# A two-layer graph kernel on one core: the first row gathers and two weight loads moved from the relation block into the projection block ahead of it

## What is computed

```
seg  = edge_type * n + dst
agg  = segment_sum(x[src], seg, num_segments=N_REL * n)
cnt  = segment_sum(ones, seg, num_segments=N_REL * n)
mean = agg.reshape(N_REL, n, -1) / maximum(cnt, 1.0).reshape(N_REL, n, 1)
h1   = einsum('rni,rio->no', mean, W_rel) + x @ W_root + b_rgcn
xw   = h1 @ W_gcn
```

## Time and profile before

| what | value |
|---|---|
| median of 3 runs | 1698.77 us (1698.74 to 1700.25) |
| the profiled execution's own time | 1700.29 us |
| its span in the trace | 1698.5 us |
| TensorE's mean granted clock | 0.861 of full |
| PE busy (matrix products) | 1337.8 us, 79% of the span |
| DVE busy | 935.5 us, 55% |
| POOL busy | 634.3 us, 37% |
| ACT busy | 535.3 us, 32% |
| 36-product groups of the relation block (L599 on r_pO) | 2592 products, 433.1 us |

### The profile page before, as it was taken

How to read it: one execution, slowest core, us unless ns; L and a number is a source line. 1 busy time by engine, 2 the same in 40 slices (tenths; PEclk the granted TensorE clock), 3 DMA queues, 4 the chain that set the end, 5 groups by cost and what they waited for, 6 DMA issues and landing times. The chain is left out here.

```text
span 1698.5 us, 31020 instructions
## 1 busy us (share of the span) xinstructions
PE 1337.8 (79%) x9640; PEld 983.5 (58%) x9641; DVE 935.5 (55%) x1715; ACT 535.3 (32%) x800; POOL 634.3 (37%) x752
## 2 busy tenths in 40 slices
PE   8699376782846599956799999999999617847988
PEld 6477366782624466845566666666666416434666
DVE  8953867784544542062466665666665145656820
ACT  0000320872221342041455554555554132022300
POOL 0077536775664000012355555555555302110000
PEclk9899595795858599968899999999999858857989
DMA  1000200001002220052899899899998545232401
GB/s 54 1 2 1 77 7 10 1 1 56 19 10 76 75 69 6 1 220 96 282 277 273 267 285 286 229 285 284 288 288 229 139 146 167 65 111 71 157 15 32
DMA packets 103970, 210.46 MB, mean 124 GB/s; under 512 B 23331, under 2 KB 48384, under 8 KB 103789
## 3 DMA queue, kind: packets, MB, share of 16 engines
q1 hardware_dynamic: 75244, 145.72, 24.7%
q0 software_dynamic: 28672, 64.04, 16.6%
HBM read 196.71 MB, written 37.22 MB: 138 GB/s over the span
## 5 line engine op out<-in xcount | busy, mean ns | idle before, releaser
L599 PE MATMUL r_pO<-ring,r_rowsT 128*128 x2592 | 433.1, 326 | 0.0
L599 PEld LDWEIGHTS r_pO<-ring,r_rowsT 128*128 128x128 f16 x2592 | 250.7, 98 | 158.4 <-issue 0.2
L1660 DVE SCALAR_TENSOR_TENSOR ring<-q_wstage,ring 128x768 f16<-128x768 f32 x198 | 175.1, 954 | 67.1 <-ACT ring L1619 65.8
L1599 POOL DMA_INDIRECT acc_dram<-r_msg,r_scol x72 | 133.7, 1858 | 169.4 <-PE r_pT L1720 109.5
L1619 ACT ACTIVATE ring<-q_wstage 128x768 f16<-128x768 f32 x198 | 148.8, 829 | 39.8 <-issue 24.9
L442 POOL DMA_INDIRECT inv_col<-qinv_dram,pair_col x112 | 120.7, 1078 | 79.3 <-POOL pair_col L455 75.2
L392 POOL DMA_INDIRECT slot_dram<-table_record,table_rowi x80 | 105.8, 1323 | 107.8 <-issue 107.2
L355 PE MATMUL acc<-oh_d,oh_s 125*125 125x512 f16 (+1 forms) x800 | 140.6, 315 | 0.0
L1648 ACT ACTIVATE r_msg<-r_pO,slot_inv 128x768 f32<-128x768 f32 x72 | 64.5, 896 | 197.0 <-PE r_pO L599 196.6
L1720 PE MATMUL r_pT<-r_S,q_parts 128*128 128x128 f16 x876 | 104.3, 222 | 26.9 <-DVE r_S L1677 10.8
L1667 DVE TENSOR_TENSOR r_rowsT<-r_pT,r_rowsT 128x512 f16<-128x512 f32 x73 | 50.3, 689 | 126.4 <-ACT r_rowsT L1628 126.4
(11 more groups left out here) (356 smaller groups left out, 2420.9 us busy)
## 6 DMA issues: line engine op xcount, KB each, us to landing
q_wstage<-in_L_gnn_W_rel_dram SPq DMA_DIRECT2D x33, 2304.0 KB, 14.3
f_stage<-in_L_ffn_w_dram SPq DMA_DIRECT2D x12, 768.0 KB, 5.2
stage<-in_L_gnn_W_dram SPq DMA_DIRECT2D x6, 768.0 KB, 6.0
q_wstage<-in_L_ffn_w_fast_dram SPq DMA_DIRECT2D x6, 768.0 KB, 5.3
q_wstage<-in_L_ffn_w_slow_dram SPq DMA_DIRECT2D x6, 768.0 KB, 7.9
q_wstage<-in_L_ffn_h_fast_dram SPq DMA_DIRECT2D x6, 768.0 KB, 9.6
f_stage<-in_L_ffn_w_fast_dram SPq DMA_DIRECT2D x6, 768.0 KB, 4.5
f_stage<-in_L_ffn_w_slow_dram SPq DMA_DIRECT2D x6, 768.0 KB, 6.0
```

The costliest lines, as they stand in the source:

```text
L599: ins = eng.matmul(out, x, w[:, h * n:(h + 1) * n], start=first and x is xh and w is wh, stop=last and x is xl, **kw)
L1599: eng.indirect_dma_start(out=K.acc_dram[u % 2], out_offset=bass.IndirectOffsetOnAxis(ap=scol[:, u:u + 1], axis=0), in_=msg[:, u, :], in_of ...
L1660: ins_ = eng.scalar_tensor_tensor(wring[:, slot, 1, k, :], wstage[:, slot, k, :], W_SCALE, wring[:, slot, 0, k, :], ALU.mult, ALU.subtract)
```

## The change

The helper functions of the relation block that load weights and gather rows move into a class `Relation`, made ahead of the projection block, with their semaphores. The four first gathers are now issued by POOL within the projection block, once the stores of `store_rows` have landed and the transposes are copied out. The loads of W_rel[1] and W_rel[2] are issued by SP within the projection block, behind the store to `xn_dram`, each when the weights that stood in its slot have been cut. The relation block starts its loads with W_rel[3]. The core of the diff:

```diff
+class Relation:
...
+    def load_w(self, eng, r, u):
...
+    def gather(self, eng, t, b):
+
+        idx = self.K.slot_idx
+        eng.tensor_copy(self.gcol[:, b, :], idx[:, t, :] if isinstance(t, int) else idx[:, bass.ds(t, 1), :].rearrange("p a b -> p (a b)")
+                        ).then_inc(self.s_col, 1)
+        eng.wait_ge(self.s_col, t + 1)
+        eng.nop(nofuse=True)
+        eng.indirect_dma_start(out=self.rows[0][:, b, :], out_offset=None, in_=self.K.xn_dram,
...
         @block.sync
         def _(eng):
             eng.dma_start(K.acc_dram[0][0:N, :].rearrange("(i p) c -> p i c", p=P), h1[:, :, :]).then_inc(s["seeded"], 16)
-            for b in range(AHEAD):
-                eng.wait_ge(gathered[b], 32)
-            load_w(eng, 1, 1)
-            with eng.Fori(1, REL // 2) as i:
+            eng.wait_ge(s["w_lo"], 2)
+            relation.load_w(eng, 3, 1)
+            with eng.Fori(2, REL // 2) as i:
                 for u in range(2):
                     eng.wait_ge(s["w_lo"], i * 2 + (u - 1))
-                    load_w(eng, i * 2 + u, u)
+                    relation.load_w(eng, i * 2 + u, u)
...
             eng.sem_inc(s["w_hi"], KC)
             eng.sem_inc(s["w_lo"], 1)
-            for b in range(AHEAD):
-                gather(b, b)
             for u in range(UN):
                 step(u, u, True)
...
             eng.wait_ge(T.s["lo_ready"], NT)
             eng.dma_start(K.xn_dram.rearrange("(i p) c -> p i c", p=P), parts[:, :, :, :].rearrange("p i a c -> p i (a c)")).then_inc(s["extra"], 16)
+            w_root.ready(eng, KC - 1)
+            relation.load_w(eng, 1, 1)
+            w_first.ready(eng, KC - 1)
+            relation.load_w(eng, 2, 0)
             eng.wait_ge(s["extra"], 32)
             eng.wait_ge(s["dumped"], 48)
 
-        def zero_seconds(eng, s):
+        def first_gathers(eng, T, s):
             eng.memset(rows_b[:, :, :], 0.0).then_inc(s["zeroed"], 1)
+            eng.wait_ge(s["dumped"], 48)
+            eng.wait_ge(s["extra"], 32)
+            T.wait_done(eng)
+            for b in range(AHEAD):
+                relation.gather(eng, b, b)
```

More of the change, by code:

```diff
@@ L1406, in _ @@
             else:
-                gpsimd(eng, s)
+                gpsimd(eng, T, s)
         @block.vector
@@ L1503, in scalar, with __init__, relation_phase @@
         eng.activation(self.parts[:, 0, c, :], self.slot(c)[:, 0, :], ACT.Copy, scale=W_SCALE).then_inc(self.s_hi, 1)
-def relation_phase(K, wstage, wring, rows_a, rows_b, h1, w_gcn, merged):
+class Relation:
+    def __init__(self, K, wstage, rows_a, rows_b, gcol):
+        self.K, self.wstage, self.rows, self.gcol = K, wstage, (rows_a, rows_b), gcol
+        self.s_staged = [K.sem("r_staged_%d" % u) for u in range(2)]
+        self.s_col = K.sem("r_col_ready")
+        self.s_gathered = [K.sem("r_gathered%d" % u) for u in range(UN)]
+    def load_w(self, eng, r, u):
+        w_rel = self.K.ins["L1_gnn_W_rel"]
+        eng.dma_start(self.wstage[:, u, :, :], w_rel[r].rearrange("(k p) n -> p k n", p=128) if isinstance(r, int) else
+                      w_rel[bass.ds(r, 1), :, :].rearrange("a (k p) n -> p (a k) n", p=128)).then_inc(self.s_staged[u], 16)
+    def gather(self, eng, t, b):
[5 more added lines that the diff above has]
+        eng.indirect_dma_start(out=self.rows[0][:, b, :], out_offset=None, in_=self.K.xn_dram,
+                               in_offset=bass.IndirectOffsetOnAxis(ap=self.gcol[:, b, 0:1], axis=0)).then_inc(self.s_gathered[b], 16)
+        eng.indirect_dma_start(out=self.rows[1][:, b, :], out_offset=None, in_=self.K.xn_dram,
+                               in_offset=bass.IndirectOffsetOnAxis(ap=self.gcol[:, b, 1:2], axis=0),
+                               bounds_check=N - 1, oob_is_err=False).then_inc(self.s_gathered[b], 16)
+def relation_phase(K, wstage, wring, relation, h1, w_gcn, merged):
     nc, ins = K.nc, K.ins
-    w_rel = ins["L1_gnn_W_rel"]
+    rows, gathered = relation.rows, relation.s_gathered
     with ExitStack() as ctx:
         sb = lambda n, s, d: K.sb(n, s, d, ctx)
-        rows = (rows_a, rows_b)
         rowsT = sb("r_rowsT", [128, 2, 2, KC, 128], FP16)
@@ L1573, in _ @@
         def _(eng):
-            def gather(t, b):
-                eng.tensor_copy(gcol[:, b, :], pair(K.slot_idx, t)).then_inc(s["col_ready"], 1)
-                eng.wait_ge(s["col_ready"], t + 1)
-                eng.nop(nofuse=True)
-                eng.indirect_dma_start(out=rows[0][:, b, :], out_offset=None, in_=K.xn_dram,
-                                       in_offset=bass.IndirectOffsetOnAxis(ap=gcol[:, b, 0:1], axis=0)).then_inc(gathered[b], 16)
-                eng.indirect_dma_start(out=rows[1][:, b, :], out_offset=None, in_=K.xn_dram,
-                                       in_offset=bass.IndirectOffsetOnAxis(ap=gcol[:, b, 1:2], axis=0),
-                                       bounds_check=N - 1, oob_is_err=False).then_inc(gathered[b], 16)
             def step(t, u, first):
@@ L1588, in step @@
                 eng.nop(nofuse=True)
-                gather(t + AHEAD, b)
+                relation.gather(eng, t + AHEAD, b)
                 if first and u == 0:
@@ L1842, in rgcn_phase @@
         merged = MergedFirst(K, wstage[:, :, :, :].rearrange("p s k n -> p s (k n)").rearrange("p s (a n) -> p s a n", a=3))
-        with ExitStack() as relation:
-            rows_b = K.sb("q_rows_b", [128, UN, 2 * C], FP16, relation)
-            project_block(K, "q1", xn, norm, xT, parts, w_root, h1, store_rows, add_bias, beside=w_first, gpsimd=zero_seconds)
+        with ExitStack() as relation_ctx:
+            rows_b = K.sb("q_rows_b", [128, UN, 2 * C], FP16, relation_ctx)
+            relation = Relation(K, wstage, rows_a, rows_b, K.sb("q_gcol", [128, UN, 2], I32, relation_ctx))
+            project_block(K, "q1", xn, norm, xT, parts, w_root, h1, store_rows, add_bias, beside=w_first, gpsimd=first_gathers)
             w_gcn = Weights(K, "q2_w", rows_view(ins["L1_gnn_W_gcn"]), wstage[:, 0], None)
-            relation_phase(K, wstage, wring, rows_a, rows_b, h1, w_gcn, merged)
+            relation_phase(K, wstage, wring, relation, h1, w_gcn, merged)
         w_gcn.parts = sb("gcn_parts", [128, 2, KC, C], FP16)
```

11 lines of the change are left out of this document (2 added, 9 removed).

## The result

The change measured **1694.42 us** (median of 12 executions, all but one disturbed one between 1681.33 and 1696.87), beside 1699.41 for the kernel before (12 executions, 1697.41 to 1703.72): a ratio of 0.9951, 95% interval 0.993 to 0.9972. So it is faster by 5 us where 19.9 were forecast, and outside the range. The time of the profiled execution is 1696.87 us, its span 1694.6.

What follows compares the result with a forecast made beforehand. PE (TensorE) was taken to bound the steady loop, so an earlier start is kept: tile 5's mean 19.9 us earlier, after term 3's 2.4 back, gives 1698.77 - 19.9 = 1678.9 us; range 1675 to 1687.

Steps and rivals of the forecast that it cites:

- Term 1: Relation block's start: with the first gathers issued early, the first mean starts 10.0 us earlier.
- Term 2: Cut of W_rel[1]: early loads remove the wait, so tile 2's products come 21.4 us earlier than before.
- Term 3: First scatter: it now waits for the store of h1, delaying tile 5's mean and giving back 2.4 us.
- rival 1: Store of h1 lands as late as before, delaying the first scatter: gain 13.1 us, 1685.7 us; chance 0.12.
- rival 2: Projection block: early loads stretch the store to xn_dram by 10.4 us: gain 15.2 us, 1683.6 us; chance 0.08.
- rival 4: Projection block: POOL's gather issues stretch beside DVE's work and end the block late: slower, 1705 us; chance 0.04.
- rival 3: Loop of relations: weight loads set the pace and swallow the head start: gain 0 to 3 us, 1698.8; chance 0.04.
- and keeps it, as nothing behind it is changed: Behind tile 5's mean: the 19.9 us gained by there last to the kernel's end.
- More than 7 us of PE waits in the loop: Loop of relations: a listed sign that the forecast is wrong.

Runs made afterwards that it cites:

- e4_other_half: The change, with tile 0 scattering into the accumulator half that the h1 store doesn't touch, and tile 1 waiting for that store instead: 1682.76 us, ratio 0.9895.
- e3: The change with only the two weight loads moved early; the gathers are issued in the relation block as in the kernel before: 1689.7 us, ratio 0.9933.
- e2: The change with only the four gathers moved early; the two weight loads go back to the relation block: 1696.1 us, ratio 0.9978.
- e7: The change with only the gathers of tiles 0 and 1 in the projection block; those of tiles 2 and 3 open the relation block: 1682.47 us, ratio 0.9896.
- e12: The change, with each loop scatter of tile t held until the high part of tile t+2 is written: 1709.15 us, ratio 1.0005.
- e14: The change with two tiles' gathers moved, tile 0 scattering into the other half, and scatters held for tile t+2's high part: 1706.46 us, ratio 0.9981.
- e15: The change with three tiles' gathers moved, tile 0 scattering into the other half, and scatters held for tile t+2's high part: 1702.86 us, ratio 0.9968.

## Why the prediction was wrong, and where it was right

**Term 1 was right.** From the block's start to the products of tile 0 it is 5.6 us, before 16.0: 10.4 won, 10.0 forecast. I had assumed that the first mean runs at the clock's lower level (1.2 GHz) from its start. It began at the higher one and was at the lower by 796, so the products start 4.5 us behind it and not 5.0, which is the 0.4:

```profile
794.00:796.00 2.00, 1.22 (x17) 1.25 (x18) 1.65 (x7) 0.00 (x0) 0.00 (x0) 0.84 0.25 91
796.00:798.00 2.00, 2.00 (x20) 1.76 (x18) 0.61 (x4) 0.86 (x2) 0.18 (x1) 0.50 0.32 120
```

**Term 2 was right.** No wait for the cut. To the products of tile 2 it is 20.8 us, before 42.0: 21.2 won, 21.4 forecast.

**Term 3 had the right mechanism and was undersized.** The first scatter came 20.0 us behind the block's start, not 17.5, since h1 took 19.1 us to land (the store's semaphore at 812.8) and not 17; the hole is 3.7 us, not 2.4. The gain at this point is 18.4 against 19.9. e4_other_half shows that nothing else makes the hole. (The terms 787.9, 14.7, 0.6 and 1.6 add up to 804.8, where the sum went on with 805.2.) By this step alone the kernel would have come out 1.5 us above my 1678.9.

**Rivals 1, 2 and 4 fell, and rival 3 as it was put.** h1 lands 19.1 us behind its issue and not 25.3 as before. What rival 1 feared from the loads was the gathers' doing: the landing takes 25.2 us in e3, with the gathers beside the store and the loads ahead of it, 18.8 in e2, with the loads beside it and the gathers ahead, and 22.7 in e7 with two tiles' gathers beside it. The store to xn_dram isn't stretched, and the gather issues of POOL in the projection block took 1.0 to 1.3 us; the price that rival 4 feared isn't seen. The loop did swallow part of the head start, as rival 3 had it, but not by loads that set the pace: PE names no load in the loop.

**The step that failed is "and keeps it, as nothing behind it is changed".** It was true of the instructions and false of two costs. First, the drain of GpSimd at the block's end, 3.7 us, which comes when the last of the four tiles' gathers is issued ahead of the block (shown by five values, and by e2 against e3). I had read the waits up to the last scatter only, and never the stretch behind it. Second, the loop: in a stretch of this trace it takes on a cadence of 15.4 us a relation instead of 14.5, worth 10 us; by their times, most executions of some series do the same, of which one each is traced. "More than 7 us of PE waits in the loop" was on my list of what would prove me wrong, and it was so: 14.3, beside 6.1 before.

**What is shown of the second, and what isn't.** That the 10 us stand where a mean's semaphores are late is read from the traces. That these arrive with the end of a scatter's issue holds for all 82. That the issue of a gather is part of it is read from the 255 and the 15 cases above, and from e12, e14 and e15: with the scatter ordered behind, the semaphores come late behind the gather alone. No version forces both to stay clear of the mean's end, so it isn't shown that the time comes back without the collision, and nothing shows how an issue on GpSimd holds a semaphore of TensorE. Open stay: why the collision starts (often near 1022 to 1040 and 1090 us), why it persists in one execution and ends in another, why the change's traces on two chips showed none, and why neither trace of the kernel before has one, though its loop is the same: in both, no gather's issue begins in the 1.05 us ahead of a mean's end behind tile 5, and what sets that isn't shown.

Without the second cost the change is worth 18.3 - 3.7 = 14.6 us; that is what three series measured (14.5, 14.5 and 16.0), and 1684.6 is still within my range. It isn't what the measured 1694.42 says.

## What to carry to other kernels

When work is moved out of a block, read also what the block's end costs: the drain of the engine that issues the DMAs, and the time to the next block's first instruction, can change though no instruction there did. Moving less can be worth more: two tiles' gathers gave nearly the same start (2.0 us later at tile 5's mean, 4.6 at tile 6's) and kept the short drain, and the best version (1678.07) came from that and from sending the first scatter to the half of the accumulator that nobody is storing to. A wait that is to end a collision has to be checked against everything else that its engine issues: here it put the gather where the scatter had been. And a loop that seems bound by one engine can hold a second cadence; a shift of its start is enough to make it matter, so repeat the measurement on more than one chip before a 0.5% result is believed.

## What the runs showed of the hardware

- GpSimd's drain at the end of a block took exactly 3.457, 3.212, 3.084, 2.962 and 7.127 us with zero, one, two, three and four tiles' gathers (two DMAs each) moved out of the block. I know no reason for the step. At the end of the projection block, behind moved gathers, the drain of the change's trace took 6.02 us.
- The semaphore of a mean's last matmul was seen 1.0 to 2.9 us late 212 times: 82 times with the end of a scatter's issue on GpSimd, which in 50 of them started 0.32 to 0.35 us after the matmul's end, behind a gather's issue; and 130 times (e12, e14, e15) some 1.65 us behind the start of a gather's issue, with no scatter. Where GpSimd issued no gather in the 1.05 us ahead of the mean's end, it came within 0.2 us in 1051 of 1079 cases.
- The store of h1 (1875 KB) landed 18.8 to 19.1 us behind its issue without the first gathers beside it, 22.7 with two tiles' and 25.2 with four tiles' beside it.
- The same kernel on the same inputs had a median of 1684.6, 1684.7, 1685.1, 1694.4 and 1694.4 us on five occasions, while the kernel before stood at 1699.1 to 1701.2, and 1699.3 on a sixth, where the kernel before stood at 1708.3.
